# A statistics finish ahead of the next statistics take, and result rows reloaded in 4, 4, 8 and 16 tiles

## The reference, cut to what matters

```python
x = x + 0.5 * _L0_ffn_ref(_layernorm(x), ...)    # top-1 of 8 experts
x = x + _L0_attn_ref(_layernorm(x), ...)         # linear recurrence over 512 steps
x = x + 0.5 * _L0_ffn_ref(_layernorm(x), ...)
x = x + 0.5 * _L1_ffn_ref(_layernorm(x), ...)    # soft mixture, 256 slots
x = x + _L1_attn_ref(_layernorm(x), ...)         # causal attention, 16 heads
x = x + 0.5 * _L1_ffn_ref(_layernorm(x), ...)
```

## Time and profile before

| | us |
|---|---|
| three runs | 924.59, 926.11, 926.19 |
| median | 926.11 |
| the profiled execution | 928.48, of which the span 926.7 |
| PE busy | 755.0 (81%) |
| DVE busy | 629.1 (68%) |
| ACT busy | 511.9 (55%) |
| POOL busy | 410.2 (44%) |

### The profile page before, as it was taken

One profiled execution on the slowest core, in us unless ns is written; L12 is line 12 of the kernel. 1 busy time (PEld: TensorE's weight loads), 2 busy tenths in 40 slices (PEclk: granted clock), 3 DMA queues, 4 the chain that ended last, 5 costly groups with the idle time before them and its releaser, 6 DMA issues.

```text
span 926.7 us, 17982 instructions
## 1 busy us (share of the span) xinstructions
PE 755.0 (81%) x5574; PEld 510.8 (55%) x5574; DVE 629.1 (68%) x2321; ACT 511.9 (55%) x1401; POOL 410.2 (44%) x536
## 2 busy tenths in 40 slices
PE   3779993798589970689696989999999998768977
PEld 2669993556389970467582333334434343356757
DVE  4465454777764438866378888888988998476634
ACT  4425542605245533676630378878878787468650
POOL 3036762401067742321073487786886843332100
PEclk9999997896589995799896599999999999879989
DMA  6741114002011113000014111221221200000003
GB/s 158 224 120 48 53 47 109 1 1 74 18 49 51 52 40 86 1 1 1 1 39 109 45 49 32 63 60 32 65 60 28 70 3 3 1 1 1 1 1 92
DMA packets 52875, 43.76 MB, mean 47 GB/s; under 512 B 9358, under 2 KB 48214, under 8 KB 52566
## 3 DMA queue, kind: packets, MB, share of 16 engines
q1 hardware_dynamic: 47134, 33.51, 13.6%
q0 software_dynamic: 4096, 8.40, 2.9%
q10 hardware_dynamic: 1552, 0.70, 0.3%
HBM read 17.35 MB, written 10.49 MB: 30 GB/s over the span
## 4 chain that ended last, share of the span: by engine, by line
PE 62%; DVE 16%; issue 9%; ACT 6%; POOL 3%; DMA 2%; ACTq 1%; DVEq 0%; SPq 0%; POOLq 0%
PE psum L820 8%; PE psum L833 8%; PE psum L1576 8%; PE psum L1561 6%; PE psum L1515 4%; PE psum L774 3%; PE psum L1380 3%; DVE half_stats L450 2%; PE psum L1280 2%; DVE x L720 2%; PE psum L1317 2%; PE psum L1289 2%; PE psum L770 2%; ACT arena L1716 2%; PE psum L1548 1%
## 5 line engine op out<-in xcount | busy, mean ns | idle before, releaser
L1648 DVE CUSTOM_DVE_ANT_0 cst<-psum,rot 128x512 bf16<-128x512 f32 (+3 forms) x512 | 217.0, 487 | 27.3 <-PE psum L1548 21.1
L1716 ACT ACTIVATE arena<-psum 128x512 f32<-128x512 f32 (+1 forms) x384 | 178.5, 533 | 41.8 <-PE psum L1561 34.8
L1548 PE MATMUL psum<-arena 64*128 64x512 bf16 (+3 forms) x512 | 123.0, 320 | 13.2 <-DMA arena<-cut 7.7
L1561 PE MATMUL psum<-arena 64*128 64x512 bf16 (+3 forms) x512 | 110.9, 304 | 9.5 <-ACT arena L1716 8.0
L746 ACT ACTIVATE arena<-psum,gate_b1T 128x128 f32<-128x128 f32 x234 | 68.8, 365 | 73.9 <-PE psum L820 73.9
L859 POOL DMA_INDIRECT arena<-xhat_rows,token_of x64 | 61.9, 967 | 105.2 <-DVE token_of L661 80.8
L1576 PE MATMUL psum<-arena 128*32 128x512 f32 (+3 forms) x1024 | 90.3, 450 | 5.9 <-POOL arena L1812 5.9
L820 PE MATMUL psum<-arena 128*128 x624 | 88.1, 286 | 4.3 <-issue 2.7
L833 PE MATMUL psum<-arena 128*128 x624 | 88.1, 285 | 0.5 <-ACT arena L746 0.5
L1809 POOL TENSOR_SCALAR_AFFINE_SELECT arena<-arena 128x384 f32<-128x384 f32 x128 | 63.6, 520 | 55.5 <-ACT arena L1716 55.0
L1561 PEld LDWEIGHTS psum<-arena 64*128 64x128 bf16 x512 | 37.3, 94 | 90.0 <-ACT arena L1716 56.6
(11 more groups left out here) (252 smaller groups left out, 1603.3 us busy)
## 6 DMA issues: line engine op xcount, KB each, us to landing
arena<-cut SPq DMA_DIRECT2D x96, 128.0 KB, 2.4
xhat_rows<-xh SPq DMA_DIRECT2D x16, 256.0 KB, 2.3
arena<-result_rows SPq DMA_DIRECT2D x8, 512.0 KB, 6.1
x<-in_L_attn_x SPq DMA_DIRECT2D x4, 512.0 KB, 7.6
arena<-in_L_ffn_w SPq DMA_DIRECT2D x1, 2048.0 KB, 9.4
out<-x SPq DMA_DIRECT2D x4, 512.0 KB, 3.2
arena<-xhat_rows,token_of POOLq DMA_INDIRECT x64, 2.5
result_rows<-arena,token_of POOLq DMA_INDIRECT x64
```

What stands on the lines that cost most here:

```text
L1548: mm = pe.matmul(to[:, col:col + (k + 1) * P], q_stack[b % STACKS][rows, h, k * P:k * P + P], k_stack[b % STACKS][rows, h, 0:(k + 1) * P], ...
L1561: mm = pe.matmul(bank[MAX_BANKS + number % EXP_BANKS][:, col:col + S - k * P], k_stack[b % STACKS][rows, h, k * P:k * P + P], q_stack[b % ...
L1648: last = nc.vector.tensor_tensor_reduce(masked_scores[:, number % 2, col:col + n_keys], frm[:, col:col + n_keys], mask[:, S - n_keys:], 1. ...
L1716: nc.scalar.activation(prob_e[g % 2][:, j, first:last], bank[MAX_BANKS + number % EXP_BANKS][:, 0:last - first], ACT.Exp, scale=DH ** -0.5 ...
```

## The change

It does two things.

In `stats_after`, for every stage but stage 0, the finish of group g-1 stands in front of the take of group g. Stage 0 keeps its order, and the last group's own finish stays behind its take.

The four transfers that bring the result rows back carry 4, 4, 8 and 16 tiles. DVE waits for a transfer in front of the first tile that it brings: ahead of tiles 0, 4, 8 and 16. The bytes and the number of transfers stay the same.

```diff
         def stats_after(dve, n, g):
 
+            if g and n:
+                stats_finish(dve, n, g - 1)
             stats_take(dve, n, g)
-            if g:
+            if g and not n:
                 stats_finish(dve, n, g - 1)
             if g == GROUPS - 1:
                 stats_finish(dve, n, g)
...
+            BACK = (0, TB, GT, 2 * GT, T)
...
                 for q in range(4):
-                    sp.dma_start(yback[:, 8 * q:8 * q + 8, :],
-                                 yrow_dram.rearrange("(t p) d -> p t d", p=P)[:, 8 * q:8 * q + 8, :]).then_inc(back[q], 16)
+                    tiles = slice(BACK[q], BACK[q + 1])
+                    sp.dma_start(yback[:, tiles, :], yrow_dram.rearrange("(t p) d -> p t d", p=P)[:, tiles, :]).then_inc(back[q], 16)
...
                 for g in range(GROUPS):
-                    dve.wait_ge(back[g], at["back"][g] + 16)
                     for t in range(GT * g, GT * g + GT):
+                        if t in BACK:
+                            q = BACK.index(t)
+                            dve.wait_ge(back[q], at["back"][q] + 16)
                         nc.vector.scalar_tensor_tensor(x[:, t, :], yback[:, t, :], prob[:, t:t + 1], x[:, t, :],
                                                        ALU.mult, ALU.add).then_inc(x_done[n + 1], 1)
```

## The result

The changed kernel takes 933.0 us (median of 4 runs, 932.3 to 933.5) where the kernel before, run beside it, takes 926.15 (4 runs, 924.6 to 926.5): a ratio of 1.0072, 95% interval 1.0058 to 1.0087. It is slower, by 6.9 us, where 9.7 were predicted. The two profiled executions differ by less, 933.04 against 928.48, because the one of before was 2.3 us above its median. So the trace can explain 4.6 us, and the runs must explain the rest.

What follows compares the result with a forecast made beforehand. It took DVE to bound the kernel in front of the recurrence and the mixture, PE in front of the second expert block. Terms 3.4 + 3.0 + 2.6 + 2.5 - 1.8 = +9.7 on 926.11 gave 935.8 us, range 929.5 to 940.5.

Steps and rivals of the forecast that it cites:

- The reload: At both ends of an expert block, the smaller first transfer gives DVE work sooner: -1.8 us (-3.8 to -0.6).
- Groups 1: In front of the recurrence and second expert block: ACT's first tile +0.2 us; ACT's group 1 +0.6 at the former.
- Group 3 at place 1: In front of the recurrence, the finish of group 2 delays ACT's group 2: +3.4 us (2.7 to 3.9).
- PE's clock at place 1: In front of the recurrence, PE stands idle and its clock falls: +3.0 us (0 to 6.0).
- Group 3 at place 2: In front of the second expert block, group 2's finish waits for group 1's store: +2.6 us (2.0 to 3.2).
- Groups 1 and 2 at place 3: In front of stage 3's mixture, finishes beside POOL delay root 2 and L999: +2.5 us (+0.9 to +3.3).
- (a): Stalls are there, but PE's clock does not fall in front of the recurrence: 932.8 us; chance 0.28.
- (b): Faster: before the recurrence and second expert block the finish finds its waits met, nothing stalls: 922.3 us; chance 0.08.
- (c): No change: stalls shortened by slack in ACT's and PE's chains, reload at its upper end: about 926 us; chance 0.07.
- (d): PE's clock, once low, stays low through the recurrence's steps: 6 us more, 942 us; chance 0.05.

Runs made afterwards that it cites:

- the kernel with ACT's order: Changed kernel with only L481 and L482 in front of the take, and ACT's root behind the previous group's tiles: 923.99 us, 0.9982 of the kernel before.

## Why the prediction was right, and where its terms were off

Direction and mechanism held at every place, and 933.0 lies in the range. The size held in part by luck: the terms came to +9.7, the profiles show them at +4.8, and the medians' 6.9 has 2.1 in it that no term explains. One thing in the working doesn't follow: the bounds of the terms, all at one end, give 927.9 to 941.9, and the stated range is narrower than that without saying why. Term by term, predicted against the profiles:

- **The reload**: -1.8 predicted, -2.7 in the profiles (1.35 and 1.37) and -2.5 by the run of it alone, inside its bounds. The step that was mis-sized is the price: the slope was taken from two stores (3.2 and 2.3 us), and the read of HBM is steeper. It matters that the saving was no more than what DVE could cover, as the kernel with two tiles shows. The Trainium skill (DMA: Bandwidth & Descriptors, Anatomy of one DMA) gives a variable part of bytes over 436 GB/s, 0.6 us for these 256 KB, for another path; the two traces, of transfers that SP issues, show more than twice that, 1.35 us.
- **Groups 1**: +0.6 for ACT's group 1 predicted at place 1, +0.09 measured (15.84 to 15.93 after the first addition). POOL does block the shift beside it, but in the kernel before it blocked an operation of the take instead (L455 took 0.80 there at 168.64). I charged the new block and did not credit the old one.
- **Group 3 at place 1**: +3.4 predicted, +2.5 measured (ACT's start 21.59 to 24.06). The parts by the timelines: L481 and L482 0.4, POOL's block 0.83 less the 0.62 that L455 lost to POOL before (0.79 at 174.40 in that trace, the next one 0.16), the wait for PE 0.6, four tiles 1.6, less 0.2 since ACT starts nearer to L464: 2.6. Two things were too large: the +0.6 carried over from group 1, and the second L912, for which I let L518 wait until its end and then take 1.12 more. In fact L518 started at 172.69, beside it, and took 1.71. 
- **PE's clock at place 1**: +3.0 predicted. It fell, and from the rows it costs 1.6 us in after, 1.2 with the new order in stage 1 alone, 2.1 in the changed kernel again and 2.3 with the order alone (the distance less 33.7, which is the 34.04 of the kernel with the gap filled less the 0.34). Here too the mechanism was right and the size was not. I charged two sets of 16 L931 and more, 3.0; in the profile of after one set pays, 3.67 where 2.05 is the full-clock time, 1.6 us, and the next is fast again:

```profile
184.62 2.05 PE L936 MATMUL psum<-xT,arena 128*128 128x128 f32 x16 [0.24 <-ACT xT L538]
```

The clock fell behind a gap of 2.9 us and did not fall when that gap was filled. The rule of the Trainium skill (TensorE: Matmul & The Clock Gate, HAM oscillation), that waits between bursts of matmuls bring the slow clock back, agrees with that.
- **Group 3 at place 2**: +2.6 predicted, +2.54 measured. The lines that show it:

```profile
221.44 3.51 POOL L856 MEMSET arena<- 128x4096 f32 x1 [37.05 <-DVE x L905]
226.11 1.11 DVE L520 TENSOR_SCALAR xh<-x,st 128x128 f32<-128x128 f32 x4 [4.41 <-DMA xhat_rows<-xh]
227.14 1.64 DVE L450 BATCH_NORM_STATS2 half_stats<-x 128x6 f32<-128x128 f32 x8
...
230.50 2.48 PE L775 MATMUL psum<-cst,xh 128*128 128x128 f32 x8 [1.86 <-ACT xh L534]
```

DVE stands 4.41 us in front of L518 for the store of group 1, and the `bn_stats` that were ready stand behind it. ACT starts 4.2 us later than before, counted from the memset (8.53 us after it, 4.30 before; 4.3 were predicted), and 2.5 of it reach the gate.
- **Groups 1 and 2 at place 3**: +2.5 predicted, +0.87 measured. After the change:

```profile
366.01 2.50 POOL L1150 TENSOR_TENSOR arena<-arena,gamma 128x512 f32<-128x512 f32 x2 [16.55 <-ACT arena L1177]
366.32 1.00 DVE L482 SCALAR_TENSOR_TENSOR st<-st 128x8 f32<-128x8 f32 x1
367.36 1.50 DVE L991 TENSOR_SCALAR arena<-x,st 128x128 f32<-128x128 f32 x2
368.78 2.35 DVE L998 TENSOR_TENSOR arena<-arena,beta 128x512 f32<-128x512 f32 x2
371.05 1.63 DVE L450 BATCH_NORM_STATS2 half_stats<-x 128x6 f32<-128x128 f32 x8
373.64 2.18 DVE L725 SCALAR_TENSOR_TENSOR x<-arena,x 128x128 f32<-128x128 f32 x8
373.77 0.21 ACT L472 ACTIVATE st<-st 128x8 f32<-128x8 f32 x1 [3.99 <-DVE st L464]
376.59 0.17 DVE L1004 TENSOR_SCALAR st<-st 128x8 f32<-128x8 f32 x1 [0.76 <-ACT st L1192]
```

All the blocks named in the prediction are there, and L720 takes 2.18 where it took 4.20. Root 2 stands 1.57 us later after the first addition (18.68, now 20.25). The step that failed is the last: "L999 needs ACT's squares". It needs them now, but before it stood behind L720, which ended at 372.20, while this line of the kernel before shows ACT done at 371.37:

```profile
371.16 0.21 ACT L1187 ACTIVATE st<-st 128x8 f32<-128x8 f32 x1
```

So 0.7 us of slack took the first part of the delay, and 1.57 - 0.7 is the 0.87 measured. The delay itself was at the low end of its range: L482, L986 and L993 lost 0.83 + 0.9 + 1.06 us, and the third take began 17.5 us after the first addition, which is the 367.4 of the prediction. Two more blocks on L993, which I had leaned to ("nearer to the blocked end since POOL asks first"), did not come.

**The rivals.** (a), no fall of the clock, gave 932.8, and the median is 933.0; but the clock did fall in each of the four profiled kernels with this order in stage 1 and no filler. The agreement is of the sum, not of the case: its clock term was absent and its other terms too large. (b) falls: at both places L518 found its waits unmet, 0.57 and 4.41 us. (c) falls with the measured loss. (d) falls: the clock was at 1.00 again by 184 to 186.

**What stays open.** The profiles explain 4.6 to 4.8 us of 6.9; the rest is the 2.3 us by which the profiled execution of before lay above its median. The part behind L999 differs from execution to execution by more than that: from L999 to a fixed instruction of the mixture (L1106) it is 95.6 us with the reload alone and 97.5 before. PE's clock is at 0.50 for the first part of this stretch and for 6.8 us near 455 in both, but in the kernel before it fell once more, for 3.4 us (two stretches of that kernel):

```profile
406.00:408.00 2.00, 1.38 (x4) 1.12 (x5) 0.00 (x0) 1.98 (x5) 0.00 (x0) 0.69 0.00 0
408.00:410.00 2.00, 2.00 (x6) 1.53 (x5) 0.69 (x1) 1.28 (x4) 0.00 (x0) 0.50 0.00 0
```

All fourteen traces fit this: the nine with such a further fall between 383 and 411 take 97.4 to 98.0 us from L999 to L1106, the five without it 95.6 to 96.5. Before and after are both among the nine, the reload alone and the order alone among the five. From L1106 to the end the traces differ by up to 3.0 us more, 454.6 to 457.6, with the same work. For the order alone these two stretches are 1.3 and 1.4 us shorter than for the changed kernel. That is where the reload's gain went in this pair of traces; one trace for each kernel can't tell whether it is so in the medians. Runs of the kernel before alone spread from 923.2 to 929.2. Whether the order of stages 1 to 3 makes such falls more frequent can't be told either. For stage 1 alone, 4.4 us by its ratio and 3.7 by its trace, the same is open.

## What to carry to other kernels

Before moving a step forward, list everything it calls: here two operations of 0.2 us were worth nothing in front, and what came along, four tiles with their two waits above all, cost 7.5 us by the traces and 8 to 9 by the medians, since DVE, which keeps its order, had ready work behind them. Ask next whether the consumer's own order lets it use the earlier signal. Split a transfer as far as the work on its first piece covers the landing of the second, and no further: here four tiles first gained 2.5 us, two tiles first nothing.

## What the runs showed of the hardware

- The landing of the first piece of result rows goes 4.20, 2.85, 2.19 us for 512, 256 and 128 KB, with three more transfers issued behind it each time. The first 256 KB taken off are worth 1.35 us, the next 128 KB 0.66: about the same price for a byte, and steeper than the stores' 0.9 for 256 KB. It scatters: from the issue to the first addition it is 4.04 to 4.22 us in the two traces with 512 KB first, 2.57 to 3.04 in the eleven with 256 KB, 2.18 and 2.20 in the one with 128 KB.
- A small DVE operation on 8 columns with two inputs in SBUF takes 1.00 us beside POOL's L912 or L1145 and 0.17 without, that is, as long as POOL's instruction still lasts. With one input in SBUF it can happen too: L458 and L464, 1.12 to 1.19 us in the kernel with ACT's order. `bn_stats` showed nothing of it (1.63 us for eight beside POOL's 1.27, as without). The Trainium skill (SBUF — State Buffer, Who interferes with whom) says that a DVE instruction with two inputs in SBUF contends with a GpSimd instruction that reads SBUF and not with one that only writes it, and that `tensor_scalar` can be of a kind where whoever comes first holds the shared ports for the whole instruction. The rows agree, also beside POOL's memset, which only writes (219.30 to 222.81 in the kernel before). There L455, with two inputs, is not held, and L458, with one, is:

```profile
220.96 0.17 DVE L455 TENSOR_TENSOR st<-half_stats 128x8 f32<-128x8 f32 x1
...
221.33 1.51 DVE L458 TENSOR_SCALAR st<-st 128x8 f32<-128x8 f32 x1
```

- The same 33.51 MB of the first hardware queue went in 44,062 packets after the change and in 47,134 before. The pieces 4, 4, 8, 16 and 2, 6, 8, 16 both give 44,062, and pieces of 8 alone give 47,134, 1,536 more in each of the two blocks. By the profile pages of both kernels 4,096 packets of under 2 KB are gone, as many as the two pieces of 16 tiles have rows of 512 B, and 1,024 larger ones came, a quarter of that. So it is this piece that goes in fewer and larger packets. No run shows what that alone is worth.
- A spell of PE's low clock at place 1 lasted 3.4 us (after; stage 1 alone) or 6.8 us (order alone; the changed kernel again), and cost an estimated 1.6 and 1.2, 2.3 and 2.1 us: about a third to a half of its length.
